# Two more fp32 products of a decoder kernel done in float32r passes, with their splits on ScalarE and VectorE

## What is computed

```python
# layer 0, feed-forward: a base product and one of four low-rank experts per token
out = einsum('bsd,od->bso', hidden, W) + b
scores = x @ gate_w.T + gate_b                      # 4 experts, ranks 8, 16, 32, 64; top 1
lora = stack([x @ A[:r, :].T @ B[:, :r].T for r in RANKS], axis=1)
x = layernorm(x + out + lora[chosen])

# layer 1, "attention": linear, weights from 4-bit codes, each with a low-rank addition of rank 16
attn = (q + k + v) / 3.0                            # each a linear map of x
x1 = x + lin(attn, dequant(codes[3], scales[3]), A[3], B[3])
g, u = lin(x1, gate weights), lin(x1, up weights)
x = layernorm(x + x1 + lin(silu(g) * u, down weights))
```

## Time and profile before

| | us |
|---|---|
| median of 3 runs | 634.55 (633.81 to 635.37) |
| profiled execution, its own time | 634.79 |
| its span, first to last instruction | 633.0 |
| mean granted TensorE clock | 0.999 of full |
| TensorE matmul busy | 620.7 |
| TensorE weight load busy | 460.6 |
| VectorE busy | 449.5 |
| ScalarE busy | 388.7 |
| GpSimd busy | 64.7 |

### The profile page before, as it was taken

How to read it: one execution, slowest core, us unless ns; L and a number is a source line. 1 busy time by engine, 2 the same in 40 slices (tenths; PEclk the granted TensorE clock), 3 DMA queues, 4 the chain that set the end, 5 groups by cost and what they waited for, 6 DMA issues and landing times.

```text
span 633.0 us, 8684 instructions
## 1 busy us (share of the span) xinstructions
PE 620.7 (98%) x3186; PEld 460.6 (73%) x3186; DVE 449.5 (71%) x718; ACT 388.7 (61%) x564; POOL 64.7 (10%) x116
## 2 busy tenths in 40 slices
PE   9999999999999999999999999999999999999996
PEld 6655555544568888878888888887777788887874
DVE  5788787557678979898987627334675777777467
ACT  2977798746677688686966136232558545667532
POOL 1032133211130000000000000001221000000012
PEclk9999999999999999999999999999999999999999
DMA  8763486302134135443630005019001133200002
GB/s 254 286 186 114 163 277 208 101 1 86 56 91 119 51 98 153 131 141 91 180 108 19 1 0 167 1 50 419 30 1 34 50 101 100 67 0 2 1 34 101
DMA packets 25777, 64.46 MB, mean 102 GB/s; under 512 B 5601, under 2 KB 10785, under 8 KB 24966
## 3 DMA queue, kind: packets, MB, share of 16 engines
q1 hardware_dynamic: 23478, 62.19, 30.6%
q10 hardware_dynamic: 2256, 1.70, 0.9%
HBM read 59.27 MB, written 4.60 MB: 101 GB/s over the span
## 4 chain that ended last, share of the span: by engine, by line
PE 80%; ACT 7%; DVE 5%; DMA 4%; issue 2%; SPq 1%; POOL 0%; POOLq 0%; DVEq 0%; ACTq 0%
PE bank L1126 19%; PE bank L1262 10%; PE bank L1114 5%; PE bank L1115 5%; PE bank L1113 5%; PE bank L965 4%; PE bank L885 4%; PE bank L689 3%; ACT line L1398 3%; DMA b_gu<-in_b_gu 2%; PE bank L995 2%; PE bank L824 2%; PE bank L1204 2%; PE bank L1205 2%; DMA codes<-in_c_qkv 1%
## 5 line engine op out<-in xcount | busy, mean ns | idle before, releaser
L1398 ACT ACTIVATE line<-line 128x1024 f32<-128x1024 f32 x87 | 91.4, 1050 | 0.1
L1113 PE MATMUL bank<-xh,wh 128*128 128x512 f32 x224 | 87.4, 390 | 0.0
L1114 PE MATMUL bank<-xl,wh 128*128 128x512 f32 x224 | 87.4, 390 | 0.0
L1115 PE MATMUL bank<-xh,wl 128*128 128x512 f32 x224 | 87.3, 390 | 0.0
L1126 PE MATMUL bank<-wh,xh 128*128 128x512 f32 x176 | 69.7, 396 | 0.2 <-DVE xl L2387 0.2
L1126 PE MATMUL bank<-wh,xl 128*128 128x512 f32 x176 | 68.6, 390 | 0.0
L2387 DVE TENSOR_TENSOR xl<-arena,xh 128x1024 fp32r<-128x1024 f32 (+1 forms) x24 | 28.3, 1179 | 35.7 <-ACT xh L1703 35.5
L1703 ACT ACTIVATE xh<-arena 128x1024 fp32r<-128x1024 f32 (+1 forms) x24 | 24.4, 1021 | 39.6 <-PE bank L1126 35.3
L1115 PEld LDWEIGHTS bank<-xh,wl 128*128 128x128 f32 x224 | 42.0, 188 | 8.8
L1113 PEld LDWEIGHTS bank<-xh,wh 128*128 128x128 f32 x224 | 42.1, 188 | 8.6
L1114 PEld LDWEIGHTS bank<-xl,wh 128*128 128x128 f32 x224 | 42.1, 188 | 8.4
(11 more groups left out here) (288 smaller groups left out, 1354.2 us busy)
## 6 DMA issues: line engine op xcount, KB each, us to landing
codes<-in_c_gu SPq DMA_DIRECT2D x14, 512.0 KB, 5.1
scales<-in_s_gu SPq DMA_DIRECT2D x28, 256.0 KB, 3.9
codes<-in_t_gu SPq DMA_DIRECT2D x8, 512.0 KB, 4.3
codes<-in_c_dn SPq DMA_DIRECT2D x7, 512.0 KB, 5.0
scales<-in_s_dn SPq DMA_DIRECT2D x14, 256.0 KB, 3.9
fold<-in_t_dn SPq DMA_DIRECT2D x1, 3584.0 KB, 15.7
codes<-in_c_qkv SPq DMA_DIRECT2D x6, 512.0 KB, 4.6
scales<-in_t_gu SPq DMA_DIRECT2D x6, 512.0 KB, 4.1
```

The costliest lines, as they stand in the source:

```text
L1113: pe.matmul(dst, wh[:, s, c:c + P], xh[:, k, cols], start=(k == 0), stop=False)
L1114: pe.matmul(dst, wh[:, s, c:c + P], xl[:, k, cols], start=False, stop=False)
L1115: last = pe.matmul(dst, wl[:, s, c:c + P], xh[:, k, cols], start=False, stop=(k == KD - 1))
L1398: nc.scalar.activation(below(slot), below(slot), ACT.Prelu, bias=bias, scale=scale, alpha=alpha).then_inc(bent, 1)
```

## The change

- `lora_out` becomes two float32r matmuls: all of `lmT_r` (rows 0 to 63 the high part of the coefficients, rows 64 to 127 their rest) with `b_hi` (the high part of B, twice), and `lmT_one` (high part again, and two rows of ones) with `b_rest` (the rest of B, and the bias as high part and rest in rows 64 and 96).
- To that end `choose` writes the masked coefficients twice, side by side; `lora_T` transposes all 128 columns; ScalarE copies out both `lmT_one` and `lmT_r`; VectorE subtracts (`lm_low`), and the count `lmT_ready` goes up by two per block. `ranks(b)` now waits for `lm_low(b - 2)` as well.
- `experts_split` on VectorE, once, ahead of `choose(0)`, makes `b_hi`, `b_rest` and the constant rows. `bT0` is loaded in four DMAs.
- `attention_product` becomes three float32r passes per pair of groups. For it ScalarE copies the high parts of `wsum` and `woT` (`rows_high(j)`) and VectorE makes the rests (`rows_low(j)`) in blocks 0 to 3.
- `PLAN[3]` goes from one unit per block to 1, 0, 1, 0, 2, 1, 2, 1; the copies and subtractions of the rank-16 stacks change places.

```diff
-PLAN = ([0] + [1] * (NT - 1), [2], [0] + [1] * 7, [1] * NT)
+PLAN = ([0] + [1] * (NT - 1), [2], [0] + [1] * 7, [1, 0, 1, 0, 2, 1, 2, 1])
...
-            sp.dma_start(bT0[0:RMAX + 1, :], i["bT0"]).then_inc(in_ffn0, 16)
+            for half in range(2):
+                sp.dma_start(bT0[half * RMAX:(half + 1) * RMAX, :], i["bT0"][0:RMAX, :]).then_inc(in_ffn0, 16)
+            for row in B_ROWS:
+                sp.dma_start(wk2[row:row + 1, :], i["bT0"][RMAX:RMAX + 1, :]).then_inc(in_ffn0, 16)
...
-                    pe.wait_ge(lmT_ready, b - 1)
+                    pe.wait_ge(lmT_ready, 2 * (b - 1))
...
-                pe.transpose(turn_bank(b)[0:RMAX, P:2 * P], lm[:, b % 2, :], ident[:, :]).then_inc(lm_ps, 1)
+                pe.transpose(turn_bank(b)[:, P:2 * P], lm[:, b % 2, :], ident[:, :]).then_inc(lm_ps, 1)
...
-                pe.wait_ge(lmT_ready, b + 1)
-                pe.matmul(bank[FF_BANK[b % 3]][:, :], lmT[0:RMAX + 1, b % 2, :], bT0[0:RMAX + 1, :], start=False, stop=True).then_inc(f0_ps, 1)
+                pe.wait_ge(lmT_ready, 2 * (b + 1))
+                dst = bank[FF_BANK[b % 3]][:, :]
+                pe.matmul(dst, lmT_r[:, b % 2, :], b_hi, start=False, stop=False)
+                pe.matmul(dst, lmT_one[0:B_ROWS[1] + 1, b % 2 * P:(b % 2 + 1) * P], b_rest[0:B_ROWS[1] + 1, :], start=False, stop=True).then_inc(f0_ps, 1)
...
-                    pe.wait_ge(af_added, 2 * KD)
+                    pe.wait_ge(af_added, 6 * KD)
...
-                    pe.matmul(dst[:, :], wsum[:, j, c * P:(c + 1) * P], woT[:, j, :], start=(j == 0), stop=False)
+                    pe.matmul(dst[:, :], w_hi[j][:, cols], wo_hi[j], start=(j == 0), stop=False)
+                    pe.matmul(dst[:, :], w_hi[j][:, cols], wo_lo[:, j, :], start=False, stop=False)
+                    pe.matmul(dst[:, :], w_lo[:, j, cols], wo_hi[j], start=False, stop=False)
...
+            def rows_high(j):
+
+                act.wait_ge(af_added, 6 * j + 2)
+                if j == 0:
+                    act.wait_ge(kq_ps, NT)
+                nc.scalar.activation(w_hi[j], wsum[:, j, :], ACT.Copy).then_inc(af_added, 1)
+                nc.scalar.activation(wo_hi[j], woT[:, j, :], ACT.Copy).then_inc(af_added, 1)
...
-                nc.scalar.activation(lmT[0:RMAX, b % 2, :], turn_bank(b)[0:RMAX, P:2 * P], ACT.Copy).then_inc(lmT_ready, 1)
+                nc.scalar.activation(lmT_one[0:RMAX, b % 2 * P:(b % 2 + 1) * P], turn_bank(b)[0:RMAX, P:2 * P], ACT.Copy)
+                nc.scalar.activation(lmT_r[:, b % 2, :], turn_bank(b)[:, P:2 * P], ACT.Copy).then_inc(lmT_ready, 1)
...
                     unit_bends(u, h)
+                if t < KD:
+                    rows_high(t)
                 if t >= 1:
                     norm_tail(2 * NT + t - 1)
...
+            def lm_low(b):
+
+                dve.wait_ge(lmT_ready, 2 * b + 1)
+                part = lmT_r[RMAX:P, b % 2, :]
+                nc.vector.tensor_tensor(part, turn_bank(b)[RMAX:P, P:2 * P], f32(part), ALU.subtract).then_inc(lmT_ready, 1)
+
+            def experts_split():
+
+                dve.wait_ge(in_ffn0, 16 * 6)
+                dve.wait_ge(cx_ps, NT)
+                nil = lm[RMAX:P, :, :].rearrange("p s c -> p (s c)")
+                link(nc.vector.memset(nil, 0.0))
+                nc.vector.tensor_copy(lmT_one[RMAX:P, :], nil)
+                for half in range(2):
+                    nc.vector.tensor_copy(b_rest[RMAX:P, half * 2 * P:(half + 1) * 2 * P], nil)
+                link(nc.vector.tensor_copy(b_hi, bT0))
+                for row in B_ROWS:
+                    nc.vector.tensor_scalar(lmT_one[row:row + 1, :], lm[row:row + 1, :, :].rearrange("p s c -> p (s c)"), 1.0, None, ALU.add)
+                    last = nc.vector.tensor_copy(b_rest[row:row + 1, :], wk2[row:row + 1, :])
+                nc.vector.tensor_tensor(b_rest[0:RMAX, :], bT0[0:RMAX, :], f32(b_hi[0:RMAX, :]), ALU.subtract)
...
+            def rows_low(j):
+
+                dve.wait_ge(af_added, 6 * j + 4)
+                nc.vector.tensor_tensor(w_lo[:, j, :], wsum[:, j, :], f32(w_hi[j]), ALU.subtract).then_inc(af_added, 1)
+                nc.vector.tensor_tensor(wo_lo[:, j, :], woT[:, j, :], f32(wo_hi[j]), ALU.subtract).then_inc(af_added, 1)
...
+            experts_split()
             choose(0)
...
                 if t >= 3:
                     x_low(2 * NT + t - 3)
+                lm_low(t)
                 for n in range(AF0 * t, min(AF0 * (t + 1), 2 * KD)):
                     add_lora(n)
-                if t in (1, 2):
-                    stack_low_of(t - 1)
+                if t in (NT - 3, NT - 2):
+                    stack_low_of(t - NT + 3)
                 for u, h in half_plan(3, t, 0):
                     unit_part(u, h)
-                if t == 4:
+                if t == 1:
                     down_stack_low()
+                if t < KD:
+                    rows_low(t)
                 if t + 2 < NT:
                     choose(t + 2)
```

More of the change, by code:

```diff
@@ L168 @@
 AF0 = 2
+B_ROWS = (RMAX, RMAX + ROWG)
 def decoder_kernel(nc, i, out):
@@ L217, in decoder_kernel @@
         m_hi = sb("m_hi", [P, KD, D], F32R)
+        with nc.sbuf_tensor("fold_r", [P, NF, D], F32R) as fold_r:
+            pass
         fold = sb("fold", [P, NF, D])
@@ L229, in decoder_kernel @@
         gate_v = sb("gate_v", [P, 2, NL + 3 * SEG])
+        with nc.sbuf_tensor("lmT_r", [P, 2, P], F32R) as lmT_r:
+            pass
         lmT = sb("lmT", [P, 2, P])
@@ L287, in decoder_kernel @@
         lora_l = wo0
-        ad_high = wh[:, :, :].rearrange("p s c -> p (s c)")[:, 0:FF]
+        ad_high = m_hi[:, :, :].rearrange("p k c -> p (k c)")[:, 0:FF]
+        w_hi = [fold_r[:, NF - 6 + n, :] for n in range(KD)]
+        wo_hi = [wh[:, n // 2, n % 2 * D:(n % 2 + 1) * D] for n in range(KD)]
+        w_lo, wo_lo = (arena_r[:, m_at:m_at + KD * D].rearrange("p (j c) -> p j c", j=KD) for m_at in (0, KD * D))
         m_lo = [arena_r[:, m_at:m_at + D] for m_at in (wk3_at, free_at, free_at + D, wo0_at)]
@@ L338, in decoder_kernel @@
         KQ_F0, CTX_SLOT = NF - 6, NF - 2
+        b_hi, b_rest = fold_r[:, CTX_SLOT, :], fold_r[:, CTX_SLOT + 1, :]
         assert at <= KQ_F0 * D
```

37 lines of the change are left out of this document (24 added, 13 removed).

## The result

The changed kernel takes 641.97 us (median of 4 runs, 641.73 to 642.17) against 634.96 for the kernel before: ratio 1.0101, 95% interval 1.0089 to 1.0114. It is slower, by 7.0 us. The forecast was 636.8, its range ended at 639.5. The profiled execution took 642.17 with a span of 640.4 us, 7.4 more than the span before; the mean granted TensorE clock is 0.993 in place of 0.999.

The account below looks back on a forecast made before the run. TensorE was taken to bound the kernel, with VectorE close behind at one place. Matmul gains of 5.6 us against 7.9 us lost to waits gave 634.55 + 2.3 = 636.8 us; own range 635.5 to 638, full range 631.5 to 639.5.

Parts of the forecast that it names:

- the four waits: TensorE waits: block 4 base product 2.6 us, first attention product 1.9, block 7 ranks 1.5, block 6 low-rank output 1.6.
- the fifth, at 130 us: Transposes of x for block 7 wait only if `experts_split` was undersized; 1.7 us at its upper bound.
- Steps 1 and 2: Base product of block 4 starts 2.1 us late, first attention product 3.7 us late, both waiting for VectorE.
- The version without it, near +1.1: Without the hold at a change of partition quadrant, `lm_low` takes 0.21 us and the sum near +1.1, no measurable change.
- Step 3: To the end of block 3: attention product gains 0.64 us, low-rank output 0.40, lateness falls to +2.65.
- step 6: Low-rank output of block 7: its `lm_low` is ready in time, 0.40 us gained, final lateness +2.3 us.
- Steps 4 and 5: Ranks of block 7 wait 1.5 us (lateness +2.55), low-rank output of block 6 waits 1.6 us (+3.1), both for `lm_low`.
- the end of the stage passes through whole: From 190 us on, the same work follows in the same order, so the 2.3 us lateness reaches the total unreduced.
- (a): Two early waits come, two late ones not, as VectorE regains distance in block 4: 633.7 us, no change; chance 0.27.
- (b): VectorE stays off TensorE's path everywhere, its new work filling only idle time: 628.9 us; chance 0.14.
- (c): More stalls than summed, from `experts_split` at its upper bound or ScalarE's four bends in block 6: 638.5 to 639.5; chance 0.13.
- (d): The passes are not shortened: at 0.43 us for both low-rank output passes the 3.2 us gain goes; lies inside (c).

Follow-up runs that it names:

- `changed_again`: The changed kernel unaltered, run again in other executions: 640.43 us, ratio 1.0083 to the kernel before.
- `stacks_later`: The changed kernel with `stack_low_of(0)` and `(1)` moved from the heads of blocks 5 and 6 to the end of block 7: 638.34 us, ratio 1.0041.
- `before_wait_short`: The kernel before with the row statistics of the norm in block 2 taken four times instead of once: 637.24 us, ratio 1.0027.
- `fill`: The changed kernel with useless TensorE matmuls (8, 8, 5 and 8) put in the places of the four waits: 640.38 us, ratio 1.0064.
- reordered list: The changed kernel's arithmetic with VectorE's and ScalarE's work put in another order, in four steps; the last version took 632.95 us, ratio 0.9961.
- `split_only`: The changed kernel with the first attention product waiting for the last rows only ahead of its last three matmuls: 638.37 us, ratio 1.0049.

## Why the prediction was wrong

Its mechanism was right, and most sizes: the four waits came where forecast, and the fifth, at 130 us, did not. Wrong was the sum, by 5.2 us, and by its own steps that is:

- **Steps 1 and 2, W(4) and M(0)**: with the late start of 1.31 taken out, lateness 1.8 (forecast 2.1) and 3.6 (3.7). The wait of W(4) was 2.40 (2.6), of M(0) 1.97 (1.9). `experts_split` took from 124.44 to 128.69, 4.25 (4.7), and `turn_norm` stayed covered. In front of the last rests that M(0) waits for, VectorE stood idle for 1.21 us until ScalarE's copy was there, as the step has it (1.15). Two figures of these steps don't add up as written: 144.90 less two L of 0.40 is 144.1 and not 144.4, and the terms behind 152.7 come to 158.9 and not to 159.1. Neither is near the size of the miss.
- **`lm_low`** took 0.29 us, and from 140.21 to 141.78 it cost 0.44 beyond the 1.13 of the instruction ahead (forecast 0.29 and 0.43). It started at the end of the one ahead and the next at its own end, 141.45 and 141.78: the held start at another quadrant, weighed in the prediction by the Trainium skill ("VectorE: DVE Perf Modes", section on two Vector instructions with no wait between them), is seen out of PSUM too; what it waited for from ScalarE was there 1.5 us earlier, at 139.96. The version without it, near +1.1, does not fit.
- **Step 3, the end of block 3: the step that failed.** Forecast +2.65, net of the start 4.2. M was to take 2.80; from M(0)'s start to R(5), with the 0.22 of the `threes` product, it took 4.66, and 3.10 in `changed_again` at the upper clock (so M itself is 2.88, a term 0.1 too small). The step took the clock of the kernel before, 0.999, as given, though it had just found a pause of TensorE of 2 us where there had been none. This term, 1.56, and the same in step 6 for W(7), 1.61, are missing: **3.2 us** in the profiled execution.
- **Steps 4 and 5, R(7) and L(6)**: waits of 1.37 (1.5) and 1.91 (1.6). The second is longer because the step left out `stack_low_of(0)`, which the change moves from block 1 to the head of block 5. Its 0.82 was subtracted where it left and added nowhere. `stacks_later` prices that: **0.6 us**. (`stack_low_of(1)`, left out as well, starts too late to matter for L(6).)
- **The start.** Everything is **1.3 us** late by 130 us, and the sum had no term for it. The two traces part at the first products. Lines 712 and 726 are the same product in the two kernels, 697 and 711 too:

The kernel before:

```profile
4.67 2.27 PE L712 MATMUL bank<-arena,early_w 128*128 128x128 f32 x16 [0.18 <-DMA arena<-in_xT]
6.78 1.03 PE L697 MATMUL bank<-fold 128*128 128x256 f32 x4
```

The changed kernel:

```profile
7.12 1.16 PE L726 MATMUL bank<-arena,early_w 128*128 128x128 f32 x8 [0.29 <-DMA arena<-in_xT]
8.12 1.03 PE L711 MATMUL bank<-fold 128*128 128x256 f32 x4
```

The kernel before in `before_wait_short`, whose edit works only at 150 us:

```profile
4.89 3.05 PE L712 MATMUL bank<-arena,early_w 128*128 128x128 f32 x16
7.77 1.03 PE L697 MATMUL bank<-fold 128*128 128x256 f32 x4
```

  TensorE waited 0.29 us for the second half of x, which landed at 7.12. The larger part is speed: eight matmuls ahead of that took 2.04 us (from 4.78), where the kernel before did all sixteen in 2.27. The clock records of the traces have the clock's first rise 3.98 us behind the first instruction in the kernel before, 6.97 in the changed kernel and 7.04 in `before_wait_short`, which does the same work as the kernel before and is 1.0 us late at line 697. From there to the stage the changed kernel loses nothing more (1.34 at 8 us, 1.31 at 130), while `before_wait_short` had regained 0.76 by 33 us. In `changed_again` the line that is at 8.12 here is at 7.25. T(1,7) lies from 129.27 to 130.86 in the other kernels, `fill` with its slow stretch aside, and at 130.34 and 130.56 in the two versions of the kernel before. So no part of the 1.3 can be shown to be the change's: two executions of the changed kernel itself are 0.84 apart at T(1,7). The kernel before ran from 633.86 to 637.52 us over 23 executions. This part is an attribution by comparison, to the clock's first rise and the landing of x, and not an experiment; why the rise comes later in one execution than in another is open.

That the end of the stage passes through whole was right: L(7) +7.85, less its 0.4, is the +7.4 of the span. Of the rivals, (a) and (b) fell with their waits; (c) had the right side, but its reasons, `experts_split` and the bends of block 6, didn't occur, and its range ended at 639.5. (d) is refuted: L's passes advance as forecast (R and L together 1.36 in place of 1.75). What (b) hoped for is nearly what the reordered list delivers up to L(7): -3.9 where 5.2 were to be had.

Put together: 634.55 + 2.3 forecast, + 0.6 (stacks), + 0.1 (M), + 3.2 (clock), + 1.3 (start) = 642.05, against 641.97. The terms behind the forecast are read from the trace whose excess they explain, so that they add up is bookkeeping and no second proof; `changed_again`, `fill`, `split_only` and `stacks_later` are what tests them, and the start has the comparison above alone. In `changed_again`, with one slow stretch in its profile and an earlier start, the excess over the executions of the kernel before that ran beside it was 5.1 and not 7.0.

## What to carry to other kernels

When a change moves work to an engine whose list is already just in time, the order of the lists decides, not their busy share: side by side the same arithmetic took 640.43 us in one order and 632.95 in another. Give a new wait of TensorE two prices: its length, and, where it is near 2 us or more, another 1.6 us in some executions, since the clock may be lowered behind it; no single wait shorter than 1.89 us had that effect here (waits of 1.59 and 1.66 had not), but two of 1.54 and 1.33 close together had. After every wait removed, look at what is late next, on every engine: here it went from VectorE's list to a copy on ScalarE, which stood behind a norm that waited for GpSimd, then to the emptying of a bank.

## What the runs showed of the hardware

- The granted clock of TensorE fell to its lower level behind waits of 1.89 to 3.1 us (W(4), M(0), L(6), O(0), and M(0) in the kernel before with its wait of 3.05), and the W or M behind it took 1.4 to 1.7 us longer. Behind the same W(4) wait of 2.4 us it fell in `changed_again` and `split_only`, and did not in the changed kernel's first profile and in `stacks_later`.
- A wait can be bridged: with 29 small matmuls without use the clock stayed up through the whole stage in the profiled execution of `fill`, though waits of up to 0.4 us were left.
- A VectorE instruction on partitions 64 to 127, between two that work from partition 0, started only at the end of the one ahead, and the next one at its own end (141.45, 141.78); between two from partition 0 the next may start 0.08 us sooner than the end (0.68 long, 0.60 apart).
- The clock's first rise came 3.98 us behind the first instruction in one execution and 7.04 in another of the same early code (the kernel before and `before_wait_short`), and the second was 1.0 us late at the first products.
- What decides in which executions a fall comes or the first rise is late was not settled.
